# A nucleus search on three engines: step one's levels by Newton and secant steps on GpSimd, with one exact level fewer on ScalarE and one interpolated pass fewer on VectorE

## The reference

```python
def _adj_from_feats(Xa, W1, W2, W3):
    logits = (Xa @ W1) @ W2 @ (Xa @ W3).T          # [N, N]
    idx = jnp.argsort(-logits, axis=1)
    vals = jnp.take_along_axis(logits, idx, axis=1)
    csum = jnp.cumsum(jax.nn.softmax(vals, axis=1), axis=1)
    k_i = jnp.sum(csum < P_NUC, axis=1) + 1        # P_NUC = 0.9
    keep = ...                                     # the k_i largest of each row
    return jax.nn.softmax(jnp.where(keep, logits, -jnp.inf), axis=1)

for s in range(2):                                 # step zero, step one
    A = _adj_from_feats(Xa, W1, W2, W3)
    Xf, Xb, Xa = Rf @ Xf, Rb @ Xb, A @ Xa
    Z = Z + (Xf @ U1[s] + Xb @ U2[s] + Xa @ U3[s])
```

## Time and profile before

| | us |
|---|---|
| median of 3 runs | 2397.59 |
| lowest, highest | 2395.61, 2397.72 |
| span of the profiled execution | 2397.4 |
| mean granted TensorE clock in it | 0.932 of full |

### The profile page before, as it was taken

The page is one execution under the profiler, slowest core; times in us unless marked ns, Lnnn a source line. Parts: engine busy times, 40 slices in busy tenths (PEclk is TensorE's granted clock), DMA queues, the critical chain, the costliest instruction groups (busy, mean ns, idle before and its releaser), DMA issues. The chain is left out here.

```text
span 2397.4 us, 33017 instructions
## 1 busy us (share of the span) xinstructions
PE 1968.8 (82%) x10002; PEld 1296.6 (54%) x10002; DVE 1946.8 (81%) x6082; ACT 1708.7 (71%) x1806; POOL 873.0 (36%) x1438
## 2 busy tenths in 40 slices
PE   2999753999999999999945979798888888888883
PEld 1555322666666666666623555565655556555552
DVE  6777657788888888888647888988888888898885
ACT  4443236888888888888437888888887888888840
POOL 2000042344444444444433353443435344343423
PEclk9999876999999999999977999999898999999996
DMA  6777221011111111111160001001010100101023
GB/s 229 280 282 289 95 97 36 28 50 50 50 50 48 50 50 46 39 43 50 41 228 18 21 21 40 21 21 41 21 40 21 41 21 21 41 21 40 20 70 125
DMA packets 65726, 167.62 MB, mean 70 GB/s; under 512 B 7037, under 2 KB 45307, under 8 KB 61947
## 3 DMA queue, kind: packets, MB, share of 16 engines
q1 hardware_dynamic: 65530, 165.43, 19.9%
HBM read 117.95 MB, written 47.45 MB: 69 GB/s over the span
## 5 line engine op out<-in xcount | busy, mean ns | idle before, releaser
L1352 PE MATMUL banks<-xa,pt 128*128 128x256 f32 x2704 | 683.3, 407 | 126.0 <-ACT pt L920 125.9
L1352 PEld LDWEIGHTS banks<-xa,pt 128*128 128x128 f32 x2704 | 533.4, 203 | 283.3 <-ACT pt L920 139.6
L896 ACT ACTIVATE junk_a<-pb_all,minus_t 128x3327 f16<-128x3327 f32 x151 | 463.9, 3072 | 150.1 <-POOLq L823 147.5
L901 ACT ACTIVATE junk_a<-pb_all,minus_t 128x3327 f16<-128x3327 f32 x151 | 463.3, 3068 | 2.6
L1398 PE MATMUL banks<-region,at 128*128 128x512 f16 x2028 | 450.4, 381 | 0.0
L808 POOL TENSOR_SCALAR over<-over,points 128x1 f32<-128x1 f32 x151 | 164.7, 1091 | 740.5 <-ACT junk_a L901 740.4
L1398 PEld LDWEIGHTS banks<-region,at 128*128 128x128 f16 x2028 | 199.5, 98 | 231.1 <-issue 6.0
L1206 DVE TENSOR_SCALAR_CACHE_REDUCE pb_all<-banks 128x1024 f32<-128x1024 f32 x260 | 210.9, 849 | 96.6 <-PE banks L1317 93.8
L1317 PE MATMUL banks<-keys,qs 64*128 64x512 f32 (+1 forms) x832 | 199.8, 576 | 90.8 <-DVE pb_all L1206 50.2
L1344 PE MATMUL banks<-ident,pb_all 128*128 128x128 f32 x1352 | 191.7, 291 | 54.5 <-DVE pb_all L1137 34.4
L1075 DVE MAX8 junk_v<-below 128x8 f32<-128x208 f32 (+1 forms) x624 | 222.5, 432 | 2.2
(11 more groups left out here) (222 smaller groups left out, 2914.1 us busy)
## 6 DMA issues: line engine op xcount, KB each, us to landing
at<-adjT_d SPq DMA_DIRECT2D x52, 832.0 KB, 4.9
region<-in_adj_dram SPq DMA_DIRECT2D x25, 1663.5 KB, 7.9
adjT_d<-at SPq DMA_DIRECT2D x26, 832.0 KB, 3.9
fb_d<-fb_sb SPq DMA_DIRECT2D x26, 256.0 KB, 2.0
region<-fb_d SPq DMA_DIRECT2D x2, 3328.0 KB, 18.1
y_d<-y_sb SPq DMA_DIRECT2D x50, 128.0 KB, 1.9
x_d<-pb_all SPq DMA_DIRECT2D x1, 3328.0 KB, 10.4
qs<-q_d SPq DMA_DIRECT2D x104, 32.0 KB, 4.2
```

What stands on the lines that cost most here:

```text
L896: nc.scalar.activation(junk_a[:, 0:w], pb[u][:, 0:w], ACT.Relu, scale=sign, bias=t, accum_out=over[u][:, 0:1])\
L901: nc.scalar.activation(junk_a[:, 0:w], pb[u][:, 0:w], ACT.Sign, scale=sign, bias=t, accum_out=over[u][:, 1:2])\
L1352: last = nc.tensor.matmul(bank[4][:, 0:D], pt[sl][:, t * P:(t + 1) * P], xa[:, t0 + t, :], start=(t0 + t == 0), stop=(t0 + t == T - 1))
```

## The change

Step one alone is changed, apart from one GpSimd instruction of `goal` that step zero no longer issues.

ScalarE runs levels 0 to 4 and no level 5. GpSimd's new function `newton` takes the place of the bisection in step one. On the rough levels and the first exact level it works out count and mass and makes a Newton step (one reciprocal as a power of -1, `ALU.pow` with the constant tile `minus_one`); on the second exact level a secant step through the last two points, which gives the third exact threshold. VectorE measures that threshold with a pass over all columns at the head of `search`, as L1023 does today for the first tile, then brackets and interpolates once; the loop over `VERIFIED` (L1059 to L1066) is gone. In the first tile ScalarE does one exact level, VectorE two, with a secant step between them. The bias of the exact levels' passes is read from `thr` with scale -1, and `minus_t` isn't written in step one. In GpSimd's order level 5 of j falls away, the rest stays. The numbers that say how far above the target to aim are changed with it.

```diff
-    ACT_BISECTIONS = (3, 3)
+    ACT_BISECTIONS = (3, 2)
     EARLY_BISECTIONS = (0, 3)
-    AIM = (6.0, 16.0)
-    CUT_AIM = (6.0, 24.0)
-    VERIFIED = (0, 1)
+    CUT_AIM = (6.0, 20.0)
+    OVERSHOOT = 20.0
+    SECANT_AIM = 12.0
     SEGMENTS = (8, 16)
     SORTED = (24, 40)
     WSUB = (N + 1) // 4
-    MARGIN = 0.45
-    MOVES = []
-    for rough, fine in zip(ROUGH, BISECTIONS):
-        half = RANGE / 2 ** (rough + 1) + (MARGIN if rough else 0.0)
-        MOVES.append([RANGE / 2 ** (e + 2) for e in range(rough)] + [half / 2 ** (e + 1) for e in range(fine)])
+    MOVES = [RANGE / 2 ** (e + 2) for e in range(BISECTIONS[0])]
     GMAX, RMAX = max(SEGMENTS), max(SORTED)
-    KMAX = 2 + max(b + v for b, v in zip(BISECTIONS, VERIFIED)) + 1
+    KMAX = 2 + max(BISECTIONS) + 1
     MOST = max(ACT_BISECTIONS)
 
 
-    FIRST_BISECTIONS = (1, 0)
+    FIRST_BISECTIONS = (1, 1)
...
                     share = nucleus_pad[:, :] if j.t == T - 1 else NUCLEUS
-                    nc.gpsimd.tensor_scalar(targets[u][:, :], mass[u][:, 0:1], share, None, ALU.mult)
-                    ch.link(nc.gpsimd.tensor_scalar(over[u][:, 5:6], mass[u][:, 0:1], (NUCLEUS - 1.0) * WSUB / N, None, ALU.mult))
+                    if first:
+                        nc.gpsimd.tensor_scalar(targets[u][:, :], mass[u][:, 0:1], share, None, ALU.mult)
+                        return
+                    ch.link(nc.gpsimd.tensor_scalar(targets[u][:, :], mass[u][:, 0:1], share, None, ALU.mult))
+                    ch.link(nc.gpsimd.tensor_tensor(over[u][:, 8:9], mass[u][:, 0:1], targets[u][:, :], ALU.subtract))
+                    ch.link(nc.gpsimd.tensor_scalar(over[u][:, 5:6], over[u][:, 8:9], WSUB / N, None, ALU.mult))
+
+                def newton(j, e):
+
+                    u, last, f = j.third, e == LEVELS[s][j.t] - 1, e - SUB
+                    o = over[u]
+                    t = rough_t[u][:, e:e + 1] if f < 0 else thr[u][:, 2 + f:3 + f]
+                    to = rough_t[u][:, e + 1:e + 2] if f < -1 else thr[u][:, 3 + f:4 + f]
+                    count, gap = o[:, 2:3], o[:, 0:1]
+                    low = o[:, 6 + f:7 + f] if f in (0, 1) else o[:, 3:4]
+                    wanted = o[:, 5:6] if f < 0 else o[:, 8:9]
+                    a, b = o[:, 9:10], o[:, 10:11]
+                    ch.link(nc.gpsimd.tensor_scalar(count, o[:, 1:2], float(WSUB if f < 0 else N), 0.5, ALU.add, ALU.mult))
+                    ch.link(nc.gpsimd.tensor_scalar(low, count, t, gap, ALU.mult, ALU.subtract))
+                    if f >= 0:
+                        ch.link(nc.gpsimd.tensor_scalar(mass[u][:, 2 + f:3 + f], low, -1.0, mass[u][:, 0:1], ALU.mult, ALU.add))
+                    if f < 1:
+                        ch.add(nc.gpsimd.tensor_scalar(count, count, low, 1e-20, ALU.mult, ALU.max))
+                        if f < 0:
+                            ch.link(nc.gpsimd.tensor_scalar(b, low, wanted, gap, ALU.subtract, ALU.mult))
+                        else:
+                            ch.add(nc.gpsimd.tensor_scalar(a, low, wanted, 2.0 * OVERSHOOT, ALU.is_ge, ALU.mult))
+                            ch.link(nc.gpsimd.tensor_scalar(b, low, wanted, 2.0, ALU.subtract, ALU.mult))
+                            ch.link(nc.gpsimd.tensor_scalar(a, a, OVERSHOOT, t, ALU.subtract, ALU.mult))
+                            ch.link(nc.gpsimd.tensor_scalar(b, b, a, gap, ALU.add, ALU.mult))
+                        ch.link(nc.gpsimd.tensor_tensor(count, count, minus_one[:, :], ALU.pow))
+                        ch.link(nc.gpsimd.tensor_scalar(b, b, count, t, ALU.mult, ALU.subtract))
+                        if f < 0:
+                            ch.link(nc.gpsimd.tensor_scalar(to, b, -1.0, 0.5, ALU.mult, ALU.min))
+                        else:
+                            ch.link(nc.gpsimd.tensor_scalar(b, b, -1.0, 1.0, ALU.mult, ALU.min))
+                            ch.link(nc.gpsimd.tensor_scalar(to, b, 1e-5, None, ALU.max))
+                    elif f == 1:
+                        ch.add(nc.gpsimd.tensor_scalar(b, t, SECANT_AIM, low, ALU.mult, ALU.subtract))
+                        ch.add(nc.gpsimd.tensor_tensor(a, t, thr[u][:, 2:3], ALU.subtract))
+                        ch.link(nc.gpsimd.tensor_tensor(low, low, o[:, 6:7], ALU.subtract))
+                        ch.add(nc.gpsimd.tensor_scalar(count, low, low, 1e-16, ALU.mult, ALU.max))
+                        ch.link(nc.gpsimd.tensor_scalar(b, b, wanted, a, ALU.add, ALU.mult))
+                        ch.link(nc.gpsimd.tensor_tensor(count, count, minus_one[:, :], ALU.pow))
+                        ch.link(nc.gpsimd.tensor_scalar(b, b, low, count, ALU.mult, ALU.mult))
+                        ch.link(nc.gpsimd.tensor_scalar(b, b, t, 1.0, ALU.add, ALU.min))
+                        ch.link(nc.gpsimd.tensor_scalar(to, b, 1e-5, None, ALU.max))
+                    pool.sem_inc(S3("point")[u], 1)
+                    if last:
+                        pool.sem_inc(S("p_ready"), 1)
...
                 def level(j, e):
 
@@ -801,30 +844,27 @@
                     u, last, f = j.third, e == LEVELS[s][j.t] - 1, e - SUB
                     if e == 0:
                         goal(j)
+                    pool.wait_ge(S3("sums")[u], levels_before(s, j.t) + e + 1)
+                    if not first:
+                        newton(j, e)
+                        return
...
-                    for e in range(EARLY, SUB + ACT_BISECTIONS[s] - 1):
+                    for e in range(EARLY, SUB + ACT_BISECTIONS[s]):
                         level(j, e)
                     if not first:
                         level(m, 0)
-                    level(j, SUB + ACT_BISECTIONS[s] - 1)
...
-                STEPS = ((), (0,), (1,), (2, 3), (4,), (5,)) if first else ((), (6, 7), (), (8, 9), (), (11,))
+                STEPS = ((), (0,), (1,), (2, 3), (4,), (5,)) if first else ((), (6, 7), (), (8, 9), (), ())
...
+                    if not first and e >= SUB:
+                        t, sign = thr[u][:, 2 + e - SUB:3 + e - SUB], -1.0
...
-                        if j.inside(T):
-                            sums(j, 10)
...
+                    if not first and i.t > 0:
+                        ch.wait()
...
+                        if not first and e < BISECTIONS[s] - 1:
+                            told, tnow, mold, mnow = th[:, 1 + e:2 + e], th[:, 2 + e:3 + e], ms[:, 1 + e:2 + e], ms[:, 2 + e:3 + e]
+                            nc.vector.tensor_tensor(frac[:, 0:1], mold, mnow, ALU.subtract)
+                            nc.vector.tensor_tensor(frac[:, 1:2], tnow, told, ALU.subtract)
+                            ch.link(nc.vector.scalar_tensor_tensor(out=frac[:, 2:3], in0=tnow, scalar=SECANT_AIM, in1=mnow, op0=ALU.mult, op1=ALU.add))
+                            nc.vector.tensor_scalar(frac[:, 3:4], frac[:, 0:1], frac[:, 0:1], 1e-16, ALU.mult, ALU.max)
+                            ch.link(nc.vector.tensor_scalar(frac[:, 2:3], frac[:, 2:3], tg, frac[:, 1:2], ALU.subtract, ALU.mult))
+                            nc.vector.tensor_scalar(frac[:, 2:3], frac[:, 2:3], frac[:, 0:1], None, ALU.mult)
+                            ch.link(nc.vector.reciprocal(frac[:, 3:4], frac[:, 3:4]))
+                            ch.link(nc.vector.scalar_tensor_tensor(out=factor[:, :], in0=frac[:, 2:3], scalar=frac[:, 3:4], in1=tnow,
+                                                                   op0=ALU.mult, op1=ALU.add))
+                            ch.link(nc.vector.tensor_scalar(th[:, 3 + e:4 + e], factor[:, :], 1e-5, 1.0, ALU.max, ALU.min))
...
-                    for v in range(VERIFIED[s]):
-                        towards(cur[:, 0:1], AIM[s])
-                        ch.link(nc.vector.scalar_tensor_tensor(out=below[:, 0:N], in0=p, scalar=cur[:, 0:1], in1=p,
-                                                               op0=ALU.is_ge, op1=ALU.mult, accum_out=cur[:, 1:2]))
-                        nc.vector.tensor_scalar(is_lower[:, :], cur[:, 1:2], tg, None, ALU.is_ge)
-                        ch.link(nc.vector.tensor_scalar(is_upper[:, :], cur[:, 1:2], tg, None, ALU.is_lt), hold=True)
-                        nc.vector.copy_predicated(lower, is_lower[:, :].to_broadcast([P, 2]), cur[:, :])
-                        ch.link(nc.vector.copy_predicated(upper, is_upper[:, :].to_broadcast([P, 2]), cur[:, :]))
                     towards(cur[:, 0:1], CUT_AIM[s])
```

More of the change, by code:

```diff
@@ L207, in gnn_program @@
     lows, highs = ends[:, 1:3], ends[:, 0:4:3]
-    lower, upper = ends[:, 0:4:2], ends[:, 1:4:2]
-    cur = sb("cur", [P, 2], f32)
-    is_lower = sb("is_lower", [P, 1], i32)
-    is_upper = sb("is_upper", [P, 1], i32)
+    cur = sb("cur", [P, 1], f32)
     frac = sb("frac", [P, 4], f32)
@@ L224, in gnn_program @@
     minus_t = [sb(f"minus_t{u}", [P, MOST], f32) for u in range(3)]
-    over = [sb(f"over{u}", [P, 8], f32) for u in range(3)]
+    over = [sb(f"over{u}", [P, 12], f32) for u in range(3)]
     unsettled = sb("unsettled", [P, 1], f32)
@@ L808, in level @@
```

(14 more changed lines are left out.)

17 lines of the change are left out of this document (5 added, 12 removed).

## The result

| | before | after |
|---|---|---|
| median of 4 runs each, us | 2397.65 | 2513.35 |
| lowest to highest | 2395.61 to 2399.72 | 2512.06 to 2514.93 |
| span of the profiled execution | 2397.4 | 2510.3 |
| mean granted TensorE clock | 0.932 | 0.921 |

The changed kernel is slower: the ratio is 1.048, its 95% interval 1.0465 to 1.0495. The forecast was 2528 us, slower, by rival A. Its span is 112.9 us longer where the sum said 131.

The account below looks back on a forecast made before the run. No engine was full; a chain of waits inside each step-one tile was taken as the bound. 24 x 5.1 = 122, first tile +6.7, last some +2: +131 on 2397.4 gave 2528 us, range 2385 to 2600.

Parts of the forecast that it names:

- rival A: Step one: GpSimd's longer levels meet VectorE's two-input passes and are held by them; 2528 us, chance 0.62.
- Step 2: GpSimd's rough level 1: fourth step caught until 15.5 us after the tile's Exp starts, power then free, 15.6 to 16.1.
- The exact level's start, +5.1 us: ScalarE begins the first exact level 28.6 us after the tile's Exp starts instead of 23.57, +5.1 us a tile.
- The rest behind the exact level, 18.19 us: From the first exact level's start to the next Exp, ScalarE passes, TensorE and VectorE stay at 18.19 us.
- The period: Time from one tile's Exp to the next in step one: 46.8 us, against 41.76 in the tile read.
- The first tile, +6.7: First tile of step one: longer levels and added work less VectorE's savings, +6.7 us in all.
- The power, 0.50: GpSimd's new power instruction on one column: assumed 0.50 us, between bounds of 0.27 and 1.03.
- The last tile, 5.1 + 2: Last tile's tail: the 5.1 us of each tile, and some +2 because the signal follows level 4's 12 steps.
- B: Rough level 1 gets out before VectorE's new pass: 2490 us or 2397, half each; chance 0.12.
- C: No locks in the way of levels 1 and 2, ScalarE's saved time counts: 37.6 us a tile, about 2306; chance 0.12.
- D: Coarser points leave rows unsettled and the settling loop runs: 2528 us and 50 more per such tile; chance 0.08.
- E: One wait replaces another, the chain having other members within 1 us: within 10 us of today, 2398; chance 0.06.

Follow-up runs that it names:

- Experiment 1: Changed kernel plus VectorE waits for GpSimd's rough levels of the next tile: both waits 2411.02 us, cut pass's wait alone 2472.26, search's wait alone 2540.76.
- Experiment 2: Changed kernel with VectorE's two-input pass on the third exact point replaced by two one-input passes and two small instructions: 2420.24 us, ratio 1.0098.
- hold_search: Changed kernel, VectorE's pass on the third exact point waits for GpSimd's rough level 1 of the next tile: 2540.76 us, ratio 1.0598.
- hold_both: Changed kernel, VectorE's third-point pass waits for the next tile's level 1 and its cut pass for level 2: 2411.02 us, ratio 1.0058.
- experiment 5: Changed kernel with two rough levels instead of three, new threshold and aims: 2385.68 us; variants 2399.36 (wait), 2658.82 (sorting 40), 2342.13 (last aims), 2401.86 (last aims, one-input passes).
- experiment 4: Kernel before, with VectorE waiting for level 1 of the next tile at the search and level 2 ahead of its verifying pass: 2415.96 us, ratio 1.0069.
- experiment 3: Kernel before, with the third exact level moved from ScalarE to VectorE, bisection and verifying pass kept: 2412.58 us, ratio 1.0064.

## Why the prediction was right, point by point

The mechanism and its three catches were right, and most sizes; two were off, in opposite directions, so that the total came closer than its terms.

- *Which three instructions are caught.* Forecast: the fourth step of level 1 by the pass that subtracts the rest (L1137, now L1182), the fifth or sixth by the new pass, the first of level 2 by the cut. All three are there. Experiment 1 shows that the catches are the cost: with the power freed and level 2's catch 0.9 us shorter, 102 of the 116 us come back. Experiment 2 shows that the kind of pass makes them, with all traces in favour of the second SBUF input. Of the other signs named, level 2's Relu waits 8.13 us (6 or more was forecast), the exact level's 2.63 (3 to 4), and the new pass waits for no signal.
- *Step 2, the power gets in before VectorE's next search: wrong.* VectorE starts L1064 0.11 us behind L1182, where I had read at most 0.5 out of the wait that the search's head had before. So the power is caught and not the step behind it, and the new pass starts at T0 + 15.12 instead of 16.1. I had said that this moves the sum by under 0.5 us; level 1 ends at 20.05 instead of 20.6.
- *The exact level's start, +5.1 us: too large.* It is +4.00. The cut pass starts at T0 + 21.07 instead of 22.3, mostly because VectorE came sooner than I read, so its catch ends at 24.8 instead of 26.1; from there to the exact level it is 2.8 us, where I had 2.5.
- *The rest behind the exact level, 18.19 us: nearly right.* It is 18.53. TensorE's second wait, which I feared for a second slow stretch, is only 0.51 us in the kernel after and the logits run at 1.00. The first products are slow (6.11 us for 14, at about half the clock), but the logits start 7.30 us behind the exact level before and after. The 0.3 us more lie between the last logits' modelled end and VectorE's last pass over them (1890.70 and 1891.00; it was 1783.78 and 1783.73); why is open. My bound for a second slow stretch was 1.9 us; `hold_search` shows one, 2.5.
- *The period.* 46.8 was forecast, 46.06 came, and the tile I counted from (41.76) is shorter than the mean before (42.16). 23 x 5.1 = 117 against 89.7 is 27.6 us too much. The sum was only 18 too high, because the first tile's term, below, was 10 too low. That part of its closeness is luck.
- *The first tile, +6.7: too small.* From its Exp to the third's it is +16.7. The second tile's Exp stands behind the first tile's exact level in ScalarE's queue, 25.3 us behind the first Exp and not 12.9. I had set VectorE's savings against that, but they don't shorten ScalarE's queue. Step one also begins 1.4 us earlier, a term that the sum didn't have.
- *The power, 0.50: right enough.* It takes 0.567 us, the median of 104.
- *The last tile, 5.1 + 2: nearly right.* It is 7.9 longer.
- *The rivals.* B (level 1 out before the new pass) needed over 1.3 us between L1137 and the pass; 0.11 decides against it. C would be the kernel with no catch in the way. No run is that kernel: `hold_both` comes nearest, with 2411, but two catches stay in it and VectorE waits instead. So C's price of 2306 is untested. D came in none of the tiles of the changed kernel, and in one or two tiles of three of experiment 5's kernels. E is refuted by the 4 us. Its premise, that the chain has other members close behind, shows in experiment 4.
- *A reading.* The stretch in the earlier trace rows is 126.20 us long, not 126.3. Nothing rests on it.

The page "SBUF — State Buffer" of the Trainium skill, section "Who interferes with whom", which said that a VectorE instruction with two SBUF inputs and a GpSimd instruction that reads SBUF shut each other out, is borne out: GpSimd's 0.38 and 0.57 us became 3.7 and 3.9, and it ran at its free durations beside L1068 with one input. The other direction shows in the kernel before:

```profile
1767.59 4.22 DVE L1070 SCALAR_TENSOR_TENSOR below<-pb_all,cur 128x3327 f32<-128x3327 f32 x1
```

```profile
1767.60 0.73 POOL L781 TENSOR_TENSOR xf_sb<-fb_sb,t 128x256 f32<-128x256 f32 x1 [0.25 <-POOL minus_t L822]
1768.29 4.11 POOL L781 TENSOR_TENSOR xb_sb<-fb_sb,t 128x256 f32<-128x256 f32 x1
```

GpSimd's first addition runs in 0.73 us and VectorE's pass takes 0.54 more than its 3.68; the second addition is then held to the pass's end. My sum counted on this direction for 0.4 us a tile. Nothing of it came in the tile shown, since the power starts inside the new pass and can't push it.

## What to carry to other kernels

Count an engine's instructions at the price they have beside their neighbours: here 128x1 instructions on GpSimd cost 0.2 to 0.6 us alone and 2.4 to 3.9 when they start inside a two-input pass of VectorE (in the tile shown), and which of them is caught shifts with every microsecond elsewhere. In this kernel the longer step paid once a whole rough level was dropped (2342 us), and before that it cost 116. Where the catches fall counted for more than their sum: 9.7 us of them a tile went with 15 us of loss in experiment 3, and 9.9 with 116 in the changed kernel. When a wait is added to dodge a catch, look at what it delays: in one place both waits gave 102 us, one of them alone cost 27, and where VectorE was nearly full the same wait lost 14.

## What the runs showed of the hardware that I hadn't expected

- GpSimd's power instruction on 128x1 takes 0.567 us (median of 104) and 0.574 in the secant step, where its other 128x1 instructions take 0.19 to 0.47 when nothing catches them.
- Where TensorE waits matters more than how long. 7.1 us ahead of 14 products cost no time in the chain, though they ran at a granted clock of 0.52; 5.8 us ahead of the logits cost 2.5 us of it.
- From the end of VectorE's pass L1182 to the start of L1064 are 0.11 us (1861.79 and 1861.90), though the program has a branch and a semaphore wait between them.
